# Grouped attention: the mask is added in VectorE's row pass, all row scaling on GpSimd, every second head copy on VectorE

## What is computed

```python
q = (h @ wq).reshape(4, 512, 16, 128)
k = (h @ wk).reshape(4, 512, 4, 128)
v = (h @ wv).reshape(4, 512, 4, 128)
q = apply_rope(q, cos, sin)
k = apply_rope(k, cos, sin)
k = jnp.repeat(k, 4, axis=2)
v = jnp.repeat(v, 4, axis=2)
scores = jnp.einsum('bqhd,bkhd->bhqk', q, k) / math.sqrt(128)
scores = jnp.where(causal[None, None], scores, jnp.finfo(scores.dtype).min)
attn = jax.nn.softmax(scores, axis=-1)
o = jnp.einsum('bhqk,bhkd->bqhd', attn, v)
```

## Time and profile before

| quantity | value |
|---|---|
| median of 3 runs | 2497.36 us (2495.06 to 2497.61) |
| profiled execution: its time | 2495.3 us |
| profiled execution: span | 2493.4 us |
| busy over the span | PE 1999.2, PEld 1567.4, DVE 1630.6, ACT 1129.0, POOL 719.3 us |
| mean granted clock of TensorE | 0.854 of 2.4 GHz |
| this stage: first matmul, last head copy starts | 1452.72, 1841.82 us |

### The profile page before, as it was taken

How to read it: one execution, slowest core, us unless ns; L and a number is a source line. 1 busy time by engine, 2 the same in 40 slices (tenths; PEclk the granted TensorE clock), 3 DMA queues, 4 the chain that set the end, 5 groups by cost and what they waited for, 6 DMA issues and landing times. The chain is left out here.

```text
span 2493.4 us, 41392 instructions
## 1 busy us (share of the span) xinstructions
PE 1999.2 (80%) x12514; PEld 1567.4 (63%) x12514; DVE 1630.6 (65%) x3442; ACT 1129.0 (45%) x2456; POOL 719.3 (29%) x777
## 2 busy tenths in 40 slices
PE   6599976399999945888668869999979608999980
PEld 3366645299999823232356647777769608999980
DVE  6344426788888876787486757777754407888865
ACT  2144441144444411777310058888853106777750
POOL 3022222155555521000144644444420140000005
PEclk9555556599999967999878989999989658999995
DMA  3511100000000016121043432322245235555523
GB/s 121 120 53 53 49 11 1 26 26 25 21 21 25 0 55 152 53 65 40 5 136 109 130 119 85 109 105 88 105 169 169 97 115 224 214 213 214 212 89 97
DMA packets 100384, 232.06 MB, mean 93 GB/s; under 512 B 14416, under 2 KB 40144, under 8 KB 95184
## 3 DMA queue, kind: packets, MB, share of 16 engines
q1 hardware_dynamic: 96080, 221.11, 26.5%
q0 software_dynamic: 3072, 8.39, 1.1%
q10 hardware_dynamic: 1152, 1.57, 0.5%
HBM read 157.63 MB, written 72.88 MB: 92 GB/s over the span
## 5 line engine op out<-in xcount | busy, mean ns | idle before, releaser
L544 POOL TENSOR_SCALAR d_att_probs<-d_att_probs,d_att_rinv 128x128 f32<-128x128 f32 (+2 forms) x192 | 177.6, 925 | 217.9 <-DVE d_att_rinv L555 217.9
L1439 DVE SCALAR_TENSOR_TENSOR b_acc<-bank,b_gates,b_acc 128x256 f32<-128x256 f32 x512 | 212.4, 477 | 41.8 <-PE bank L1354 41.8
L1407 POOL TENSOR_TENSOR b_moe_act_low<-b_moe_act,b_moe_act_high 128x512 fp32r<-128x512 f32 x136 | 175.9, 1293 | 177.5 <-ACT b_moe_act_high L1384 177.5
L434 PE MATMUL wide<-d_att_k,d_att_q 128*128 128x128 f32 (+3 forms) x512 | 186.6, 447 | 16.2 <-DMA d_att_k<-k_dram 16.1
L2020 PE MATMUL wide<-e_moe_hT_high,e_moe_w_high 128*128 128x256 f32 x644 | 183.5, 285 | 13.0 <-DVE e_moe_w_low L2090 13.0
L913 DVE TENSOR_REDUCE a_att_rmax<-wide 128x2 f32<-128x256 f32 (+3 forms) x128 | 104.4, 823 | 131.3 <-PE wide L706 130.9
L913 DVE TENSOR_REDUCE c_att_rmax<-wide 128x2 f32<-128x1024 f32 x128 | 155.2, 1223 | 49.8 <-PE wide L698 44.6
L2020 PE MATMUL wide<-e_moe_hT_high,e_moe_w_low 128*128 128x256 f32 x644 | 183.3, 285 | 0.0
L2020 PE MATMUL wide<-e_moe_hT_low,e_moe_w_high 128*128 128x256 f32 x644 | 183.3, 285 | 0.0
L491 ACT ACTIVATE d_att_probs<-wide,d_att_nmax 128x128 f32<-128x128 f32 (+3 forms) x256 | 135.4, 529 | 76.0 <-DVE d_att_nmax L550 76.0
L2090 DVE TENSOR_TENSOR e_moe_w_low<-e_moe_w,e_moe_w_high 128x768 fp32r<-128x768 f32 x161 | 151.2, 954 | 21.0 <-ACT e_moe_w_high L2050 18.5
(11 more groups left out here) (358 smaller groups left out, 5996.2 us busy)
## 6 DMA issues: line engine op xcount, KB each, us to landing
e_moe_w<-in_e_w SPq DMA_DIRECT2D x23, 2688.0 KB, 9.4
q_dram<-d_in_rot SPq DMA_DIRECT2D x64, 256.0 KB, 3.6
d_att_q<-q_dram SPq DMA_DIRECT2D x16, 1024.0 KB, 5.1
o_dram<-d_att_o SPq DMA_DIRECT2D x64, 256.0 KB, 2.0
d_out_oT<-o_dram SPq DMA_DIRECT2D x16, 1024.0 KB, 5.6
b_moe_w<-in_b_w SPq DMA_DIRECT2D x17, 512.0 KB, 3.5
a_q<-q_parts SPq DMA_DIRECT2D x96, 64.0 KB, 2.2
c_q<-q_parts SPq DMA_DIRECT2D x96, 64.0 KB, 2.2
```

The lines of the kernel that those rows point to most:

```text
L434: nc.tensor.matmul(stile[qt], qs[s][:, u, qt * P:(qt + 1) * P], ks[s][:, 0, 0:w], start=True, stop=False)
L544: g.tensor_scalar(tile, tile, rinv[:, j, qt:qt + 1], None, ALU.mult).then_inc(scaled, 1)
L1407: g.tensor_tensor(ap[1][:, u % 4, :], act[:, u % 4, :], ap[0][:, u % 4, :], ALU.subtract).then_inc(act_low, 1)
L1439: nc.vector.scalar_tensor_tensor(out=tile, in0=y, scalar=gate, in1=tile, op0=ALU.mult, op1=ALU.add).then_inc(acc_done, 1)
```

## The change

Five things are changed, all in `grouped_attention` but for one sign.

The four mask matmuls of a step are gone. A tile `later` in SBUF holds 384 columns of zeros and the negated mask. The factor on q in the rotation table has its sign turned, so that the matmul gives negated scores; one VectorE operation (`tensor_tensor_reduce`, L546) adds `later`, writes the sum back to the PSUM tile and takes the row minimum, which is the negated maximum. It compiles into two instructions, the operation and the readout of its accumulator (both are printed as ISA below). The exponential takes the tile with scale -1.

The reciprocals are taken in pairs, two in a step: tiles 0 and 1 of step n+1 behind the low part of (n, 2), and tiles 2 and 3 of step n behind the minimum of (n+1, 0). ScalarE's scaling of tile 3 is gone, and GpSimd scales all four tiles, in the order 0 to 3. The head copy of odd steps is VectorE's (L557), with a semaphore for each of the two slots.

```diff
+        later = sb("later", [P, S])
...
-                    nc.tensor.matmul(stile[qt], qs[s][:, u, qt * P:(qt + 1) * P], ks[s][:, 0, 0:w], start=True, stop=False)
-
-                    nc.tensor.matmul(stile[qt][:, w - P:w], c.identb[:, :], c.causal[:, :], start=False, stop=True).then_inc(scores_done, 1)
+                    nc.tensor.matmul(stile[qt], qs[s][:, u, qt * P:(qt + 1) * P], ks[s][:, 0, 0:w], start=True, stop=True).then_inc(scores_done, 1)
...
-                        if qt < NQ - 1:
-                            pe.wait_ge(scaled, (NQ - 1) * n + qt + 1)
-                        else:
-                            pe.wait_ge(last_scaled, n + 1)
-
+                        pe.wait_ge(scaled, NQ * n + qt + 1)
...
-                                         bias=nmax[:, j, qt:qt + 1], accum_out=rsum[:, j, qt:qt + 1]).then_inc(exp_done, 1)
+                                         bias=nmax[:, j, qt:qt + 1], scale=-1.0, accum_out=rsum[:, j, qt:qt + 1]).then_inc(exp_done, 1)
...
-                        if qt == 0:
-                            a.wait_ge(rinv_ready, NQ * n + NQ)
-                            tile = probs[j % 2][:, NQ - 1, :]
-                            nc.scalar.activation(tile, tile, ACT.Copy, scale=rinv[:, j, NQ - 1:NQ]).then_inc(last_scaled, 1)
                         if not (last and j == 7):
                             exponentials(*back(m, j, -1), qt)
-                        if qt == 0 and not (first and j < 2):
+                        if qt == 0 and j % 2 == 0 and not (first and j < 2):
                             keep(*back(m, j, 2))
...
+                g.memset(later[:, 0:S - P], 0.0).then_inc(zeroed, 1)
                 with g.Fori(0, STEPS // 8) as m:
                     for j in range(8):
-                        for qt in range(NQ - 1):
-                            g.wait_ge(rinv_ready, NQ * (8 * m + j) + qt + 1)
-                            hold(g, spare)
+                        for qt in range(NQ):
+                            g.wait_ge(rinv_ready, 2 * (8 * m + j) + (qt // 2 + 1))
+                            hold(g, spare_g)
                             tile = probs[j % 2][:, qt, 0:width[qt]]
                             g.tensor_scalar(tile, tile, rinv[:, j, qt:qt + 1], None, ALU.mult).then_inc(scaled, 1)
 
             @block.vector
             def _(v):
-                def negated_max(m, j, qt):
+                def masked_minimum(m, j, qt):
+
                     v.wait_ge(scores_done, NQ * (8 * m + j) + qt + 1)
-                    nc.vector.tensor_reduce(nmax[:, j, qt:qt + 1], stile[qt], AX.X, ALU.max,
-                                            negate=True).then_inc(max_ready, 1)
-
-                def reciprocal(m, j, qt):
-                    v.wait_ge(exp_done, NQ * (8 * m + j) + qt + 1)
-                    nc.vector.reciprocal(rinv[:, j, qt:qt + 1], rsum[:, j, qt:qt + 1]).then_inc(rinv_ready, 1)
+                    hold(v, spare_v)
+                    nc.vector.tensor_tensor_reduce(stile[qt], stile[qt], later[:, S - width[qt]:S], 1.0, 3e38, ALU.add, ALU.min,
+                                                   nmax[:, j, qt:qt + 1]).then_inc(max_ready, 1)
+
+                def reciprocals(m, j, half):
+                    v.wait_ge(exp_done, NQ * (8 * m + j) + (2 * half + 2))
+                    pair = slice(2 * half, 2 * half + 2)
+                    nc.vector.reciprocal(rinv[:, j, pair], rsum[:, j, pair]).then_inc(rinv_ready, 1)
...
+                def keep(m, j):
+                    v.wait_ge(pv_done, 8 * m + (j + 1))
+                    v.wait_ge(o_free[1], 16 * (4 * m + j // 2 + 1))
+                    nc.vector.tensor_copy(o_slot[1][:, :], obank[1][:, :]).then_inc(o_ready[1], 1)
...
+                    following = not (last and j == 7)
                     for qt in range(NQ):
-                        if not (last and j == 7):
-                            negated_max(*back(m, j, -1), qt)
+                        if following:
+                            masked_minimum(*back(m, j, -1), qt)
+                        if qt == 0:
+                            reciprocals(m, j, 1)
                         v.wait_ge(high_ready, NQ * (8 * m + j) + qt + 1)
                         nc.vector.tensor_tensor(by_key(pT[j % 2][1], qt), turned_tile(qt), by_key(pT[j % 2][0], qt),
                                                 ALU.subtract).then_inc(low_ready, 1)
-                        if not (last and j == 7):
-                            reciprocal(*back(m, j, -1), qt)
+                        if qt == 0 and j % 2 and not (first and j < 2):
+                            keep(*back(m, j, 2))
+                        if qt == 2 and following:
+                            reciprocals(*back(m, j, -1), 0)
                     if j == 1:
                         low_values(2 * m + 1, 1)
                     if j == 5 and not last:
                         low_values(2 * m + 2, 0)
...
+                nc.vector.tensor_scalar(later[:, S - P:S], c.causal[:, :], -1.0, None, ALU.mult).then_inc(later_ready, 1)
+                v.wait_ge(later_ready, 1)
+                v.wait_ge(zeroed, 1)
                 for qt in range(NQ):
-                    negated_max(0, 0, qt)
-                for qt in range(NQ):
-                    reciprocal(0, 0, qt)
+                    masked_minimum(0, 0, qt)
+                reciprocals(0, 0, 0)
...
-    rope = np.stack([rope / np.sqrt(GD), rope], axis=1).astype(np.float32)
+    rope = np.stack([rope / -np.sqrt(GD), rope], axis=1).astype(np.float32)
```

More of the change, by code:

```diff
@@ L374, in grouped_attention @@
         o_slot = [sb(f"o{i}", [P, S]) for i in range(2)]
+        later = sb("later", [P, S])
         loaded = [sem("loaded0"), sem("loaded1")]
         o_free = [sem("o_free0"), sem("o_free1")]
-        scores_done, max_ready, exp_done, scaled, turned, high_ready, low_ready, v_high, v_low, pv_done, o_ready, rinv_ready, last_scaled, spare = (
-            sem(n) for n in ("scores", "max", "exp", "scaled", "turned", "high", "low", "v_high", "v_low", "pv", "o", "rinv", "last_scaled", "carry"))
+        o_ready = [sem("o_ready0"), sem("o_ready1")]
+        scores_done, max_ready, exp_done, scaled, turned, high_ready, low_ready, v_high, v_low, pv_done, rinv_ready = (
+            sem(n) for n in ("scores", "max", "exp", "scaled", "turned", "high", "low", "v_high", "v_low", "pv", "rinv"))
+        zeroed, later_ready, spare_a, spare_g, spare_v = (sem(n) for n in ("zeroed", "later_ready", "carry_a", "carry_g", "carry_v"))
         stile, ttile = ([c.bank[3 * i + k][:, 0:width[qt]] for qt, k in enumerate((0, 1, 0, 2))] for i in range(2))
@@ L401, in load_quad, with store @@
                                      ).then_inc(loaded[s], 16)
-                def store(n, j):
-                    sp.wait_ge(o_ready, n + 3)
+                def store(m, n, j):
+                    sp.wait_ge(o_ready[j % 2], 4 * m + (j // 2 + 2))
                     sp.dma_start(out[bass.ds(n, 1), :, :].rearrange("a p s -> p (a s)"), o_slot[j % 2][:, :]).then_inc(o_free[j % 2], 16)
@@ L413, in _ @@
                     for j in range(8):
-                        store(8 * m + (j - 8), j)
+                        store(m - 1, 8 * m + (j - 8), j)
                         if j in (2, 6):
@@ L419, in _ @@
                 for j in range(8):
-                    store(56 + j, j)
+                    store(7, 56 + j, j)
                 for i in range(2):
@@ L442, in values @@
                         pe.wait_ge(low_ready, NQ * n + NQ + 4)
-                        pe.wait_ge(o_ready, n + 1)
+                        pe.wait_ge(o_ready[j % 2], 4 * m + (j // 2 + 1))
                         if j % 4 == 0:
@@ L473, in _ @@
                 pe.sem_inc(low_ready, NQ)
-                pe.sem_inc(o_ready, 2)
+                for i in range(2):
+                    pe.sem_inc(o_ready[i], 1)
                 for qt in range(NQ):
@@ L496, in keep @@
                     a.wait_ge(o_free[j % 2], 16 * (4 * m + j // 2 + 1))
-                    nc.scalar.copy(o_slot[j % 2][:, :], obank[j % 2][:, :]).then_inc(o_ready, 1)
+                    nc.scalar.copy(o_slot[j % 2][:, :], obank[j % 2][:, :]).then_inc(o_ready[0], 1)
                 def high_values(quad, s, used):
@@ L501, in high_values @@
                         a.wait_ge(pv_done, used)
-                    hold(a, spare)
+                    hold(a, spare_a)
                     nc.scalar.copy(vq[s][0][:, :, :], vals[:, bass.ds(quad, 1), :, :].rearrange("p a k d -> p (a k) d")).then_inc(v_high, 1)
@@ L533, in _ @@
                 keep(7, 6)
-                keep(7, 7)
             @block.gpsimd
             def _(g):
+                g.memset(later[:, 0:S - P], 0.0).then_inc(zeroed, 1)
                 with g.Fori(0, STEPS // 8) as m:
                     for j in range(8):
-                        for qt in range(NQ - 1):
-                            g.wait_ge(rinv_ready, NQ * (8 * m + j) + qt + 1)
-                            hold(g, spare)
```

(4 more changed lines are left out.)

## The result

The kernel with the change takes 2563.03 us (median of 4 runs, 2550.29 to 2564.88), the kernel before on the same chip 2496.21 (4 runs, 2490.98 to 2497.61). The ratio is 1.0261, with a 95% interval of 1.0224 to 1.0297: slower, by 66.8 us where 44.7 were forecast. The profiled execution has a span of 2562.1 us and took 2563.78.

What follows compares the result with a forecast made beforehand. A ring across engines through GpSimd's scaling was taken as the bound: 63 x 6.26 = 394.4 us, conversions 22.8 and branches 2.1 put the attention stage's end 44.7 us later, giving 2540.0 us, range 2524 to 2574.

Steps and rivals of the forecast that it cites:

- The ring through GpSimd, TensorE, VectorE and ScalarE: Attention step: scaling of tiles 2 and 3, transposes, next step's scores, minimum, exponential, reciprocal, back to scaling; 6.26 us.
- TensorE, busy 96% of the time, set the pace before: Attention stage before the change: TensorE, busy 364.77 of 378 us, was taken as the bound, 5.99 us a step.
- I take the minimum to last as long as the maximum did: VectorE's fused mask and minimum, 512 columns: as long as the maximum, 0.69 us; until the exponential starts 0.73.
- The wake of TensorE: From the end of GpSimd's scaling to the start of TensorE's transposes, claimed 0.06 us.
- The conversions: VectorE's value conversion, once in four steps, delays the pair's reciprocal on the ring by 1.52 us; 15 times, 22.8 us.
- The branch of VectorE's loop: Once in eight steps VectorE's loop branch delays the pair's reciprocal; 0.3 us x 7 = 2.1 us.
- A fused operation at half rate or with a second pass: Rival, 10%: tile 3's minimum on VectorE takes up to 0.55 us longer, 35 us more, 2575 us.
- The faster case: Rival, 6%: TensorE stays the bound and the removed mask matmuls save 26 us, 2469 us.
- That the clock falls: Rival, 3%: TensorE loses the higher clock level, transposes and scores double, 92 us, above 2630 us.
- ScalarE's freed time: ScalarE without tile 3's scaling and half of the copies: hidden, since ScalarE waits in the ring.
- The saved mask matmuls: TensorE without mask matmuls: at most 0.4 us a step, 26 us, gained only if TensorE remained the bound.
- GpSimd's waits: Sign of being right: GpSimd's total waits drop from 200 us to some 60 to 120.

Runs made afterwards that it cites:

- after_scalar3: Changed kernel with tile 3 scaled by ScalarE again, reciprocals still in pairs; 2559.68 us.
- before_pairs: Kernel before with only the reciprocals joined in pairs, placed where the change puts them; 2546.43 us.
- after_reduce: Changed kernel, pairs kept, with a plain minimum in place of the fused operation and the mask left out; 2550.65 us.
- before_gpsimd3: Kernel before with only the scaling of tile 3 moved to GpSimd; 2490.52 us.
- before_copies: Kernel before with only the head copies of odd steps moved to VectorE; 2496.80 us.
- separate_reduce: Changed kernel with a reciprocal for each tile, a plain minimum in place of the fused operation and the mask left out; 2477.06 us.
- reduce_semaphore: Changed kernel with plain minimum, mask left out, pairs kept, and the semaphore increment put back ahead of the minimum; 2551.38 us.
- after_late_conv: Changed kernel with VectorE's value conversion moved behind the low part of tile 0 of the next step; 2533.01 us.

## Why the prediction was right, and where its sizes were off

**The bound and the mechanism: right.** The ring through GpSimd, TensorE, VectorE and ScalarE is the bound; TensorE waits for tile 2; tiles 2 and 3 run back to back. One point of the wording was too narrow. It put the cause on tile 3 standing behind tile 2 on GpSimd. after_scalar3 takes it away and changes nothing, because a second ring, in which tile 3's transposes stand behind tile 2's on TensorE, is as long. before_pairs shows the cause: one reciprocal for both tiles, worth 48 us alone with its place behind the conversion. The fused operation is worth 12.4 us more in the paired ring (after_reduce). By the periods of the profiles the two are 56.4 and 12.9 us of 64.9. Neither pair of numbers adds up exactly: the medians carry what varies ahead of the stage, and the periods the falls of the clock.

One premise was not right as it stood, though nothing in the sum hung on it: that TensorE, busy 96% of the time, set the pace before. In before_gpsimd3 the same TensorE work, masks included, fits into an ordinary period of 5.44 to 5.53 us instead of 5.80, once ScalarE's scaling no longer stands ahead of the exponential of tile 0. So the 96% held time in which TensorE was held up: between 1462 and 1835 us its weight loads waited 9.8 us, in 42 waits, for exponentials.

**The ring's terms: too small by 0.28 us.** Read from the rows of after, against the forecast:

| term | forecast | measured |
|---|---|---|
| tiles 2 and 3 on GpSimd | 2.81 | 2.79 |
| end on GpSimd to transposes | 0.06 | 0.13 |
| transposes to scores | 0.44 | 0.44 |
| scores to minimum | 1.05 | 1.21 |
| minimum to exponential | 0.73 | 0.80 |
| exponential to reciprocal | 0.81 | 0.80 |
| reciprocal to GpSimd | 0.36 | 0.37 |
| period | 6.26 | 6.54 |

The step that was mis-sized is "I take the minimum to last as long as the maximum did". It does (0.700 us), but it starts 0.16 later and its result is there 0.07 later. after_reduce gives 0.14 and 0.08 of this back. The wake of TensorE came from a single row of the stage's first steps and is twice that in the steady part.

**The sum.** The forecast was 44.7 us for the stage, measured 66.4. The periods give 63 x 0.285 = 18 more. The conversions cost 15 x 1.46 = 21.9 instead of 22.8. The branch of VectorE's loop costs nothing, where I had 2.1: its periods are as long as the others. Then 439.21 - 63 x 6.55 - 21.9 = 4.7 us are left. Four periods with a stretch at the lower clock are together 5.6 us longer than 6.55 (the first, and those with the falls: 1702 to 1714 above, 0.83 and 0.88; 0.72 in 1510 to 1516 and in 1846 to 1852); those of the first and last eight steps are a little shorter. From the first matmul to the first scaling of tile 2 it takes 9.11 us instead of 7.5, 1.6 more. Of this 1.0 us is there when the first minimum of 512 columns starts (5.54 us behind the first matmul against 4.52 before), likely since the clock was still at the lower level. Together 44.7 + 18 - 0.9 - 2.1 + 4.7 + 1.6 = 66.0, the rest is rounding.

**The rivals.** A fused operation at half rate or with a second pass did not come: 1.37 ns per column with all fixed cost at 512 columns, as for the maximum. The rule of the Trainium skill that was weighed ("Vector Engine (DVE) Microarchitecture Reference", section "Points that are easy to get wrong") speaks of two SBUF sources, so these rows do not test it. With one operand in PSUM, the trace shows no halved rate, and the 0.55 us did not come. The faster case was excluded by the ring, as argued. That the clock falls was priced as all or nothing; it came as short falls and a late rise, 5.6 us in four periods and likely 1 us ahead of them.

**The parts at nothing.** The copies cost nothing (before_copies). ScalarE's freed time did not show in the changed kernel: after_scalar3, which gives it the scaling back, is 3 us away from it, inside the ranges. The saved mask matmuls were worth nothing in the changed kernel, where TensorE waits in each step. In separate_reduce they may be worth something, as said above.

**What would show it.** GpSimd's waits should have dropped to 60 to 120 us and measured 178.8. I had counted only the wait ahead of tile 2, and that is 88.0. The other 90.7 are ahead of tile 0, whose reciprocal now comes with tile 1's. It costs nothing, for it isn't on the ring. TensorE's wait ahead of tile 2 is mostly 0.73 us in ordinary steps, where 0.8 or more were forecast; the periods are 6.55 and 8.00 us against 6.26 and about 7.8; and the clock was not 1.00 throughout.

## What to carry to other kernels

Joining two small operations into one saves time on their own engine (the pair of reciprocals takes 0.17 us, a single one 0.16), but the first consumer then waits for the last producer: before it is done, follow who waits for the first half, and whether that closes a ring across engines from one step to the next. When no engine is busy nearly all the time, as here with TensorE at 81%, sum such a ring from rows of the steady part and take each wake-up from there, since 0.07 us left out 63 times is 4 us. An operation that takes work off the busiest engine is worth only what its own engine's place in a ring allows, so try each part alone: here one part gained a little, one was worth nothing and two cost.

## What was not expected of the hardware

A semaphore increment that an engine issues ahead of its next operation delayed that operation by 0.10 us (reduce_semaphore, 1.17 against 1.07), even though the engine idled 0.7 us before it. The accumulator's read behind the fused operation shows as 0.142 us, but the reader of its result starts only 0.08 later than behind a plain reduction.

The granted clock fell to its lower level three times in the steady part of the changed kernel, for 3 to 4 us each (0.57 in 1511 to 1515, 1705.5 to 1709.5 and 1845.5 to 1849.5), and each time made a period 1.3 to 1.6 us longer. Each fall began 1.1 to 1.4 us behind the end of one of the 15 long waits of TensorE in conversion steps (2.0 to 2.2 us); behind the other 12 it did not fall. In after_late_conv those waits are gone, and so are the falls. But such waits alone do not bring a fall: before_pairs has 14 of them behind 1472 us, 1.9 to 2.0 us long, and its clock is 1.00 from 1472 to 1882. Each kernel has one profile, so what decides stays open, and so does why the clock rose 10 us later in the stage than before.
